# Query folded about the middle, x read mirrored, sums of q times k on VectorE, and x plus attention output formed in the dense layer

## The reference

```
x = x + tanh(g_xattn) * autocorrelation(layernorm(x), ctx, ctx)
x = x + tanh(g_ffn) * ffn(layernorm(x))
  autocorrelation: corr = ifft(fft(q) * conj(fft(k))).real over the positions
                   w, idx = top_k(corr, 12);  w = softmax(w)
                   out[t] = sum_i w_i * v[min(idx_i + t, 511)]
  ffn: x @ W_base.T + b_base + 2 * sum over 8 experts of w_e * (x @ A_e.T) @ B_e.T
       w_e from softmax(x @ W_gate.T) less a threshold, cut at zero, normalised
```

## Time and profile before

| | |
|---|---|
| median of 3 runs | 3030.74 us (3028.44 to 3033.55) |
| profiled execution, its time | 3031.29 us |
| its span in the trace | 3029.5 us |
| PE busy, share of the span | 96% |
| attention stage | to about 1442 us |
| weights phase | to about 1500 us |
| dense stage | the rest, 32 tiles |

### The profile page before, as it was taken

The page is one execution under the profiler, slowest core; times in us unless marked ns, Lnnn a source line. Parts: engine busy times, 40 slices in busy tenths (PEclk is TensorE's granted clock), DMA queues, the critical chain, the costliest instruction groups (busy, mean ns, idle before and its releaser), DMA issues.

```text
span 3029.5 us, 37059 instructions
## 1 busy us (share of the span) xinstructions
PE 2921.9 (96%) x13184; PEld 1466.0 (48%) x13184; DVE 1606.0 (53%) x2738; ACT 1012.6 (33%) x1672; POOL 1454.0 (48%) x577
## 2 busy tenths in 40 slices
PE   4999999999999999997799999999999999999999
PEld 2445554555545554553644444444444444444444
DVE  3899989999999999998722121121211112111111
ACT  4555556555555545441511121111211112111110
POOL 4788888889888888884031211212112121221210
PEclk8999999999999999999899999999999999999999
DMA  8455544555455554423634132331323313233230
GB/s 201 124 123 126 139 110 118 127 132 125 115 122 125 135 117 102 101 73 111 237 98 111 56 111 75 91 111 55 111 72 94 106 60 111 69 97 99 68 97 28
DMA packets 260355, 324.49 MB, mean 107 GB/s; under 512 B 162911, under 2 KB 163487, under 8 KB 245541
## 3 DMA queue, kind: packets, MB, share of 16 engines
q1 hardware_dynamic: 259922, 323.38, 40.1%
q10 hardware_dynamic: 348, 0.18, 0.0%
HBM read 223.76 MB, written 67.21 MB: 96 GB/s over the span
## 4 chain that ended last, share of the span: by engine, by line
PE 84%; DVE 5%; POOL 3%; issue 2%; DMA 2%; ACT 1%; SPq 1%; ACTq 0%; DVEq 0%; POOLq 0%
PE bank L1097 43%; PE bank L488 7%; PE bank L422 7%; PE bank L454 6%; PE bank L472 5%; PE bank L460 3%; POOL spec_o L869 3%; DVE rows_mem L1256 2%; PE bank L1086 1%; PE bank L1087 1%; PE bank L1088 1%; ACT wt L548 1%; PE bank L435 1%; PE bank L405 1%; PE bank L411 1%
## 5 line engine op out<-in xcount | busy, mean ns | idle before, releaser
L1281 POOL TENSOR_TENSOR rows_mem<-norm,rows_mem 128x2048 f16<-128x2048 f32 x31 | 126.1, 4068 | 1220.7 <-ACT rows_mem L1156 1220.7
L1097 PE MATMUL bank<-w_hi,rows_mem 128*128 128x512 f16 x2048 | 489.3, 379 | 3.8 <-DVE rows_mem L1256 3.8
L1097 PE MATMUL bank<-w_hi,xres_mem 128*128 128x512 f16 x2048 | 489.0, 379 | 3.5 <-DVE rows_mem L1256 3.5
L869 POOL TENSOR_TENSOR spec_o<-spec_o,term 128x1024 f32<-128x1024 f32 x190 | 443.3, 2362 | 40.6 <-DVE term L686 40.6
L1249 DVE TENSOR_TENSOR hwt_lo<-bank,hwt_hi 128x128 f16<-128x128 f32 x32 | 9.3, 292 | 790.4 <-ACT hwt_hi L1175 790.4
L1097 PEld LDWEIGHTS bank<-w_hi,rows_mem 128*128 128x128 f16 x2048 | 200.2, 98 | 251.6 <-DVE rows_mem L1256 13.6
L1097 PEld LDWEIGHTS bank<-w_hi,xres_mem 128*128 128x128 f16 x2048 | 200.2, 98 | 250.6 <-DVE rows_mem L1256 12.7
L488 PE MATMUL bank<-spec_o,table 128*128 128x512 f32 x512 | 249.1, 617 | 19.9 <-POOL spec_o L869 15.8
L1097 PE MATMUL bank<-w_lo,xres_mem 128*128 128x512 f16 x1024 | 262.8, 379 | 0.0
L1097 PE MATMUL bank<-w_lo,rows_mem 128*128 128x512 f16 x1024 | 262.8, 379 | 0.0
L422 PE MATMUL bank<-rows_mem,table 128*128 128x512 f32 x512 | 227.7, 598 | 18.0 <-POOL rows_mem L849 15.7
(11 more groups left out here) (182 smaller groups left out, 4876.3 us busy)
## 6 DMA issues: line engine op xcount, KB each, us to landing
rows_mem<-in_x_dram SPq DMA_DIRECT2D x32, 1024.0 KB, 13.0
norm<-x_scratch SPq DMA_DIRECT2D x32, 1024.0 KB, 5.5
rows_mem<-x_scratch SPq DMA_DIRECT2D x32, 1024.0 KB, 7.0
out_dram<-rows_mem SPq DMA_DIRECT2D x32, 1024.0 KB, 4.4
norm<-in_x_dram SPq DMA_DIRECT2D x28, 1024.0 KB, 10.8
rows_mem<-in_ctx_dram SPq DMA_DIRECT2D x256, 64.0 KB
rows_mem<-in_ctx_dram SPq DMA_DIRECT2D x64, 256.0 KB
xres_mem<-in_x_dram SPq DMA_DIRECT2D x256, 64.0 KB
```

Source lines behind the costliest of these rows:

```text
L869: pool.tensor_tensor(to, to, buffer, sign).then_inc(term_added, 1)
L1097: mm = pe.matmul(dense[o][:, :], nt(par, part)[:, k, :], w[:, k, o * 512:(o + 1) * 512], start=(k == 0 and n == 0), stop=False)
L1281: pool.tensor_tensor(norm_lo, norm[:, :], norm_hi, ALU.subtract).then_inc(norm_lo_made, 1)
```

## The change

- **q:** x is loaded mirrored like v (10 transfers in place of 1), folded twice on POOL (`fold_q`: 4 additions in place of 2; for step 0 on DVE) into `q_sym`, and `q_spectra` needs 4 matmuls in place of 8, with the table of v. It stands one step earlier: `q_spectra(i+1)` lies between the two output tiles of step i.
- **q times k:** two of the four products are written back to PSUM, and the sums of `sum_qk` move from POOL to DVE. Both `w_spectra` and `correlate` now wait for these sums (`q_used`).
- **x plus output:** `residual` on DVE, `load_res` and the mirrored stores go. ACT copies the two halves of the output, times the gate, to `kept` (`keep_out`), and one transfer stores them to `part_scratch`. The dense stage forms x2: it loads x and the cosine half, POOL adds (`form`), SP loads the sine half into the same buffer `addend`, POOL adds again, and SP stores x2 to be loaded again into `row`, of which there is one now. Its tiles follow the mirrored order of the positions. `form(i+3)` is worked on during tile i.
- **The first x** (batch 0) is loaded as whole rows of 2048. The first tile of the dense stage is formed, and its statistics made, during the last attention step (`first_tile`, `statistics(dve, 0)`).
- **Statistics of x** are loaded mirrored too (10 transfers in place of 1 per step).

```diff
                 def q_spectra(i, four):
-                    pe.wait_ge(q_folded, 2 * (i + 1))
+                    pe.wait_ge(q_folded, 4 * (i + 1))
                     for half in range(2):
                         pe.wait_ge(v_copied, 4 * i + 3 + half)
                         for row in range(2):
-                            for j in range(2):
-                                mm = pe.matmul(pair(four, half)[:, row, :], q_tab[:, 2 * half + row, j, :],
-                                               qf[:, 2 * row + j, :], start=(j == 0), stop=(j == 1))
+                            mm = pe.matmul(pair(four, half)[:, row, :], v_tab[:, 2 * half + row, :],
+                                           q_sym[:, 2 * half + row, :], start=True, stop=True)
...
                 def turn_w(c, four):
                     for y in range(2):
                         if least(c) >= 1:
-                            pe.wait_ge(sine_added, 4 * (c - 1) + 2 * (y + 1))
+                            pe.wait_ge(out_kept, 2 * (c - 1) + y + 1)
...
+                def keep_out(c, four, h):
+                    if h == 1 and least(c) >= 1:
+                        act.wait_ge(parts_stored, 16 * c)
+                    act.wait_ge(out_made, 2 * c + 2 - h)
+                    act.activation(kept[:, h, :, :], pair(four, 1 - h), ACT.Copy, scale=gates[:, 0:1]).then_inc(out_kept, 1)
...
+                    if least(i) >= 1:
+                        keep_out(i - 1, mine, 1)
                     if most(i) < STEPS:
                         scale_w(i)
+                    if least(i) >= 1:
+                        keep_out(i - 1, mine, 0)
...
+            def fold_q(eng, i):
+                if least(i) >= 1:
+                    eng.wait_ge(q_made, 2 * i)
+                eng.wait_ge(x_normed, 4 * (i + 1))
+                eng.tensor_tensor(qf[:, 0:2, :], xt[:, 0:4:2, :], xt[:, 1:4:2, :], ALU.add).then_inc(q_folded, 1)
+                eng.tensor_tensor(qf[:, 2:4, :], xt[:, 0:4:2, :], xt[:, 1:4:2, :], ALU.subtract).then_inc(q_folded, 1)
+                eng.wait_ge(q_folded, 4 * i + 2)
+                eng.tensor_tensor(q_sym[:, 0:2, :], qf[:, 0:4:2, :], qf[:, 1:4:2, :], ALU.add).then_inc(q_folded, 1)
+                eng.tensor_tensor(q_sym[:, 2:4, :], qf[:, 0:4:2, :], qf[:, 1:4:2, :], ALU.subtract).then_inc(q_folded, 1)
...
                 def step(i, par, phase):
+                    if most(i) == STEPS - 1:
+                        pool.wait_ge(w_made, 4 * i)
+                        first_tile()
...
+                def form(i, par):
+                    load_norm(i, par)
+                    load_sine(i)
+                    keep_x2(i)
...
                 def load(i, par):
-                    if fleast(i) >= 2:
-                        sp.wait_ge(out_stored[par], 16 * (i // 2))
+                    if fleast(i) >= 1:
+                        sp.wait_ge(out_stored[1 - par], (128, 16)[1 - par] * ((i - 1) // 2 + 1))
+                    sp.wait_ge(x2_kept, 16 * (i + 1))
...
-                load_norm(1)
+                form(1, 1)
                 load(0, 0)
+                form(2, 0)
                 for i in range(ROWS):
                     step(i, i % 2)
...
+                def form(i, par):
+                    pool.wait_ge(norm_loaded[par], (144 * (i // 2), 32 * (i // 2 + 1))[par])
+                    pool.tensor_tensor(norm[:, :], norm[:, :], addend, ALU.add).then_inc(formed, 1)
+                    pool.wait_ge(sine_loaded, 16 * i)
+                    pool.tensor_tensor(norm[:, :], norm[:, :], addend, (ALU.add, ALU.subtract)[par]).then_inc(formed, 1)
```

334 lines of the change are left out of this document (163 added, 171 removed).

## The result

| | before | after |
|---|---|---|
| median | 3029.6 us (3026.6 to 3033.6, 4 runs) | 3298.6 us (3297.9 to 3300.2, 4 runs) |
| ratio after to before | | 1.089, 95% interval 1.087 to 1.091 |
| span of the profiled execution | 3029.5 us | 3296.1 us |
| PE busy, share of the span | 96% | 88% |

The forecast was 2963. The table cuts both traces at the same places of the program. `w_spectra` is L454 before and L438 after, the turn of hw (`turn_hw`) L1105 and L1128.

What follows compares the result with a forecast made beforehand. PE was taken as the bound, with DVE and POOL close behind. 3031.3 - 1 (start) - 82.3 (attention) + 1 (last step) - 8.5 (weights) + 22 (dense start) = 2962.5, given as 2963 us against 3030.7; range 2935 to 2996.

Steps and rivals of the forecast that it cites:

- The dense tiles: Dense stage after its start: SP catches up 2.9 us a tile, tiles stay at 47.48 us, change 0.
- SP's ring: Dense tiles: SP's loop of issues and waits, store to store, 47 us or 42.2, mean 44.6, under the tile's 47.48.
- SP's ring is longer than a tile: Dense-tile rival: at 52 us a tile, +131, 3094 us; chance 0.06 for over 50, 0.06 for 47.5 to 50.
- another rule of that page: Dense transfers: advice for one transfer over 128 partitions, since pieces share the same 16 engines; speaks against the eight pieces.
- The attention step: 29 attention steps: q halved on PE, period 39.2 us, seven waits of 2.0; 1150.8 against 1233.1, -82.3 us.
- POOL's ring: Attention step: POOL's next start at 53.7 us, its result needed at 54.7, so it just fits the 39.2 period.
- my first rival: POOL and DVE take over the attention step: period 40.5, +38, 3001 us, PE waiting for `spec_o` from POOL; chance 0.12.
- those seven: Attention steps with `variance` and `scales`: first sum of q times k comes late, PE waits 2.0 us in each.
- The last step: Last attention step: `statistics(0)` ahead of `largest(31)` costs 4.3 us, missing `residual` gives back 3.2; +1 us.
- The start: Start to `w_spectra(1)`: more SP issues against an earlier `normalise(0)` and earlier q; -1 us, ends -6 and +6.
- The weights phase: After the attention steps: one store instead of ten issues lets the fifth weight tile land earlier; -8.5 us.
- The start of the dense stage: Ahead of `logits(1)`: PE stands still for 19 us, then ACT's delay and lower clock; +22 us, ends +14 and +26.

Runs made afterwards that it cites:

- the combined kernel: Changed kernel plus reordered dense stage, statistics first, DVE's steps written out, two exponentials in PSUM, `statistics(0)` cut in two: 3019.5 us; with a wait ahead of `fold_v(1)`, 3017.7.

## Why the prediction was wrong

**The dense tiles, the step that failed.** I put SP's ring at 47 and 42.2 us, mean 44.6, under the tile's 47.48, and so wrote 0; it is 52.3 and 57.6, and the tiles lost 216 us. The rival "SP's ring is longer than a tile" happened, at a mean of 54.9, where it had 0.06. Two terms of the ring in one piece were too low: the store, 4.8 in the sum, takes 10.7, and x with the cosine half, 7.2 in the sum, takes 16.4.

Of these 15.1 us, 9.9 come from the outer count: with 8 runs of 16 reversed rows the share of the DMA engines is one half, with 16 runs 0.95. The Trainium skill ("DMA: Bandwidth & Descriptors", Why a DMA increments its semaphore by 16 and not by 1) states this: the largest number up to 16 that divides the slowest dimension of both sides is the number of engines. By that, 8, and the shares of 0.50 and 0.49 agree. I had used another rule of that page, against many pieces; here the one piece was the slow form.

The other 5.2 us, and 3.9 of x in eight pieces (12.6, not 8.7), I put down to transfers that run beside one another; no run takes that apart. I took a second megabyte for half a landing more in the load, and for nothing in the store, where x2's store had been issued 0.4 us ahead. The 2.3 us that the prediction worked out for a last piece of 128 KB was low as well: in the changed kernel the pieces of the output land after 3.0 us in the median and those of x after 5.3. The section of the Trainium skill ("DMA: Bandwidth & Descriptors", Anatomy of one DMA) that the prediction used is on transfers that GpSimd issues; SP issues these.

The engine count alone would not have saved the forecast: the run without it still took 3152 us. The order of SP's queue cost more, since the ring falls under the tile once the store's landing lies beside the load (3078 us, with both slow transfers kept). Of a tile's 7.2 us, 5.2 are PE's stop and 2.0 the clock behind it, for which I had no term in a tile.

**The attention step.** Forecast 29 x 39.2 + 14 = 1150.8 us, measured 1208.4. The plain step was sized rightly: with the obstacles away it takes 39.2, though the 29 steps still take 1169.2 there. The step that failed is POOL's ring, "it just fits": I read POOL as a queue with its own work, and let `select` run beside it. An instruction of DVE with both inputs in SBUF does not run beside an addition of POOL (2.77 us in the changed kernel, 2.82 without POOL's wait, 0.75 with an input in PSUM). The Trainium skill ("SBUF — State Buffer", Who interferes with whom) has it as a lock on a shared pair of ports; the trace agrees. POOL has the same 16 additions as before, and a ring of 40.3 would lie hidden under a step of 42.5; with q halved on PE it comes to light. It costs 29 x 1.1 = 33 us. That is nearly the number of my first rival (40.5, chance 0.12), but not its sign: PE does not wait for `spec_o` from POOL, it waits for the sums of q times k from DVE, 19 times between 180 and 1380 us and not seven times.

Second, the forecast has no term for the turn of DVE's loop. Before, `residual`, 5.5 us of queued work without waits, stood ahead of the jump, and DVE stood idle for at most 0.8 us; I booked its removal as pure gain. The jump now shows, 3.24 us, with 2.3 of clock behind it, once in four steps. That `residual` hid it is read from the two traces; no run puts such work back. The Trainium skill ("Runtime: NRT & Kernel Launch", Instruction fetch mechanics) says that a taken branch can wait for its code to be fetched; written out, the wait is gone, but what DVE does in it no row shows. The gain was 15.7 us over 29 steps, less than the five stops and their clock (27), since the steps with `variance` then stop PE in their place. In the combined kernel those seven cost 3.7 us each in place of the 2.0 of the forecast.

**The last step.** +1 forecast, +8.4 measured (+6.7 with the 46.6 of most runs): three of the small instructions, priced at 0.2, took 2.1 to 2.3 beside POOL's additions. Moved away, the step is 38.4.

**The start.** -1 forecast, +38 measured. "x as whole rows lets `normalise(0)` run some 6 us earlier" was wrong in sign: the reversed half comes in two blocks with an outer count of 8, and x was complete 18 us later; in plain order, 6 us later. I counted the issues on SP's queue but not who waits behind `load_x(1)`, whose wait is for work that hangs on x. The last 5 of the 38 us are within the spread of the start.

**Right.** The weights phase (-8.3 for -8.5) and PE's work in a step. The start of the dense stage was right in kind, one stop ahead of `logits(1)`, and too small: 30.3 us for 19, by x of tile 1 in one piece (15.8 us with its half, not 7.3) and x of tile 2 in eight (12.5, not 8.7).

## What to carry to other kernels

Before an edit takes work off an engine, ask what that work was hiding: a jump, an instruction that must run alone, a landing. When a ring of waits is within a few per cent of the bound, price each of its transfers with what runs beside it, and look at the outer count of its pattern. In this hand-written queue, moving the store beside the load gave 221 us, and making the slow transfers fast 147.

## What the runs showed of the hardware that I had not expected

- A 1 MB transfer with an outer count of 8 holds the share of the 16 DMA engines at one half: 16.4 us to the next addition, 9.7 with a count of 16. In the load, reversed rows cost nothing that shows (16.4 us with either order).
- DVE's two-input instructions from SBUF and POOL's additions exclude each other down to one element a partition: 2.26 us for one that takes 0.16. One input in PSUM is enough to be free of it.
- The turn of a hardware loop cost DVE 3.24 us where nothing was queued ahead of it, 0.8 where 5.5 us of work was.
